# Linear attention and a top-2 expert layer on one Trainium2 core: the last batch and the first expert tiles reordered, output sends put off in the first wave

## The reference

```python
scores = softmax(xn @ gate_w + gate_b)                # per token, 8 experts; the two best are kept
for i in range(n_exp):
    h = relu(xn * w_i @ w1[i] + b1[i])                # 128 -> 512
    y = h @ w2[i] + b2[i]                             # 512 -> 128
    out = where(w_i > 0, y, out)                      # the last chosen expert overwrites
x = x + out
```

## Time and profile before

| | |
|---|---|
| median of three runs | 274.76 us |
| the profiled execution | 274.99 us, of which the span of its instructions is 273.0 us |
| PE busy | 245.6 us (90%), mean granted clock 0.989 |
| DVE, ACT, POOL busy | 195.5, 169.9, 166.0 us |
| DMA queues | 40.57 MB, mean 149 GB/s |

### The profile page before, as it was taken

The page is one execution under the profiler, slowest core; times in us unless marked ns, Lnnn a source line. Parts: engine busy times, 40 slices in busy tenths (PEclk is TensorE's granted clock), DMA queues, the critical chain, the costliest instruction groups (busy, mean ns, idle before and its releaser), DMA issues.

```text
span 273.0 us, 8984 instructions
## 1 busy us (share of the span) xinstructions
PE 245.6 (90%) x3045; PEld 199.5 (73%) x3045; DVE 195.5 (72%) x711; ACT 169.9 (62%) x315; POOL 166.0 (61%) x190
## 2 busy tenths in 40 slices
PE   0989999999999999999999999666998999999993
PEld 0666777777777767767767767435998999999993
DVE  4643466787799899899799798759878655555562
ACT  1386767767767767767777776544456556556550
POOL 6263364564786786786677667850477775455454
PEclk9999999999999999999999999998999999999998
DMA  5799999999600000000000000456666489777500
GB/s 152 227 342 353 352 356 352 352 335 357 196 25 22 2 22 21 2 23 22 2 20 23 2 22 20 116 134 175 185 166 169 119 241 283 180 211 178 150 29 9
DMA packets 31692, 40.57 MB, mean 149 GB/s; under 512 B 3442, under 2 KB 24468, under 8 KB 31648
## 3 DMA queue, kind: packets, MB, share of 16 engines
q1 hardware_dynamic: 29120, 35.69, 43.9%
q0 software_dynamic: 2272, 4.25, 4.5%
q10 hardware_dynamic: 256, 0.07, 0.1%
HBM read 17.98 MB, written 22.48 MB: 148 GB/s over the span
## 4 chain that ended last, share of the span: by engine, by line
PE 69%; ACT 16%; POOL 5%; issue 4%; DVE 3%; DMA 1%; SPq 0%; DVEq 0%; ACTq 0%; POOLq 0%
PE sc L1068 33%; PE p L1068 24%; ACT scores L416 16%; PE av L1068 9%; PE p L1071 3%; POOL expert_rows L594 2%; POOL scores L566 2%; DMA rows<-in_L_attn_hidden_states 1%; POOL out L607 1%; DVE scaled L768 0%; POOL rstd L583 0%; DVE logit L770 0%; DVEq L296 0%; DVE u_sb L718 0%; DVE xn L662 0%
## 5 line engine op out<-in xcount | busy, mean ns | idle before, releaser
L416 ACT ACTIVATE scores<-sc 128x1536 f32<-128x1536 f32 x64 | 92.8, 1451 | 47.0 <-PE sc L1068 47.0
L566 POOL TENSOR_SCALAR_AFFINE_SELECT scores<-scores 128x1024 f32<-128x1024 f32 x64 | 71.3, 1115 | 47.7 <-ACT scores L416 47.1
L1068 PE MATMUL sc<-q_sb,k_sb 32*128 32x256 f32 (+1 forms) x1024 | 60.9, 350 | 10.9 <-ACT scores L416 7.4
L1068 PEld LDWEIGHTS sc<-q_sb,k_sb 32*128 32x128 f32 x1024 | 48.5, 186 | 28.5 <-issue 18.3
L607 POOL DMA_INDIRECT out<-y_sb,xr x39 | 38.4, 983 | 27.6 <-DVE y_sb L1009 22.5
L1068 PE MATMUL av<-scores,v_ext 128*32 128x256 f32 (+1 forms) x1024 | 48.7, 329 | 0.9 <-POOL scores L566 0.9
L516 ACT ACTIVATE hT<-sc,b_sb 128x128 f32<-128x128 f32 x78 | 24.6, 364 | 35.7 <-PE sc L1068 34.9
L1068 PE MATMUL sc<-xwT,w_t 128*128 128x128 f32 x312 | 42.0, 279 | 0.0
L1068 PEld LDWEIGHTS av<-scores,v_ext 128*32 128x32 f32 x1024 | 28.8, 110 | 16.2 <-POOL scores L566 1.4
L997 DVE TENSOR_SCALAR hT<-sc,b_sb 128x128 f32<-128x128 f32 x78 | 23.8, 347 | 21.6 <-PE sc L1068 18.4
L594 POOL DMA_INDIRECT expert_rows<-rows,slot_i x32 | 32.8, 1024 | 10.7 <-issue 7.3
(11 more groups left out here) (136 smaller groups left out, 322.9 us busy)
## 6 DMA issues: line engine op xcount, KB each, us to landing
expert_rows<-pad_rows SPq DMA_DIRECT2D x11, 1572.0 KB, 18.3
w_t<-in_L_ffn_w SPq DMA_DIRECT2D x39, 256.0 KB, 3.5
xr<-expert_rows SPq DMA_DIRECT2D x39, 65.5 KB, 2.7
rows<-in_L_attn_hidden_states SPq DMA_DIRECT2D x16, 128.0 KB, 3.2
out<-y_sb,xr POOLq DMA_INDIRECT x39, 3.0
b_sb<-in_L_ffn_b SPq DMA_DIRECT2D x1, 512.0 KB, 5.8
expert_rows<-rows,slot_i POOLq DMA_INDIRECT x32, 2.4
wo_sb<-in_L_attn_Wo ACTq DMA_DIRECT2D x8, 8.0 KB, 2.4
```

Source lines behind the costliest of these rows:

```text
L416: nc.scalar.activation(scores[g][:, :, :, :].rearrange("p c a t -> p c (a t)"), sc[:, :, 0:SW], ACT.Square, scale=Q_SCALE).then_inc(square ...
L566: nc.gpsimd.affine_select(out=scores[g][:, :, 0:2, :], in_=scores[g][:, :, 0:2, :], compare_op=ALU.is_ge, fill=0.0, base=0, pattern=[[0, G ...
L1068: return nc.tensor.matmul(o, lhsT=l, rhs=r, start=start, stop=stop)
```

## The change

The constants become Y = 20 and DEFER = 12. In the first 12 tiles DVE no longer adds the second bias ahead: `end_y` adds the residual straight from xr, and the bias of tile t - 12 is added (`add_bias`) in the turn of tile t, for t = 12 to 23. POOL sends the results of tiles 0 to 11 only after that, interleaved with those of tiles 12 and up. In the first wave (t < 17) ACT takes three of the four relu chunks and DVE one, and `go_up` writes them to the banks accordingly. In the last period POOL runs the scatters of batches 10 and 11 and `norm2_root(6)` ahead of the four masks of batch 15; DVE and PE load the first table earlier; DVE runs the logits of pair 6 after the loop; PE runs four filler products and puts all four `weigh(15)` behind `project_o(14)`. `project_o(15)` moves from tile 0 to behind the transpose of tile 1, the two last `prefix` from tiles 1 and 6 to 4 and 8, and the late pieces are spread over tiles 0 to 11.

```diff
-    XR, W1, Y, XWT = 20, 6, 10, 4
+    XR, W1, Y, XWT = 20, 6, 20, 4
+    DEFER = 12
+        def low(t):
+            return FC - 1 if t < WAVE else FC // 2
...
 # scalar
-                if p == NB:
-                    exponent(NP - 2)
-                for c in range(FC // 2):
+                for c in range(low(t)):
             normalise(2)
+            exponent(NP - 2)
             act.wait_ge(b1_ready, 1)
-                if t == 3:
+                if t == 4:
                     exponent(NP - 1)
 # gpsimd
             def send_result(t):
-                pool.wait_ge(y_ready, t + 1)
+                if t < DEFER:
+                    pool.wait_ge(y_late, t + 1)
+                else:
+                    pool.wait_ge(y_ready, t + 1)
...
                 if p == NB:
                     scatter(send)
+                    scatter(send + 1)
+                    norm2_root(logits)
                 if core is not None:
                     mask(core, 0)
-                if p == NB:
-                    scatter(send + 1)
...
-            scatter(NB - 4)
-            scatter(NB - 3)
-            for t in range(TILES):
-                if t == 6:
-                    scatter(NB - 2)
-                    scatter(NB - 1)
-                send_result(t)
+            for b in range(NB - 4, NB):
+                scatter(b)
+            for t in range(DEFER, TILES + 1):
+                if t - DEFER < DEFER:
+                    send_result(t - DEFER)
+                if t > DEFER:
+                    send_result(t - 1)
 # vector
                     norm2_stats(tail)
+                if p == NB:
+                    e = experts(dve, 0)
...
-                if logits is not None:
+                if logits is not None and p < NB:
...
             def end_y(t):
                 dve.wait_ge(down_done, t + 1)
-                dve.wait_ge(y_begun, t + 1)
-                nc.vector.tensor_tensor(y_sb[t % Y][:, :], down_bank[t % 2][:, 0:D], y_sb[t % Y][:, :],
+                if t < DEFER:
+                    begun = xr[t % XR][:, 0:D]
+                else:
+                    dve.wait_ge(y_begun, t - DEFER + 1)
+                    begun = y_sb[t % Y][:, :]
+                nc.vector.tensor_tensor(y_sb[t % Y][:, :], down_bank[t % 2][:, 0:D], begun,
                                         ALU.add).then_inc(y_ready, 1)
+            def add_bias(t, e):
+                dve.wait_ge(y_ready, t + 1)
+                nc.vector.tensor_tensor(y_sb[t % Y][:, :], y_sb[t % Y][:, :], b2_sb[:, bass.ds(e * D, D)],
+                                        ALU.add).then_inc(y_late, 1)
...
-            e = experts(dve, 0)
+            route_logits(NP - 2)
             residual(NB - 2)
-            route_sum(NP - 2)
+            norm2_stats(NB - 2)
             spread(NB - 1)
             divide(NB - 1)
-            route_score(NP - 2)
-            route_onehot(NP - 2)
-            norm2_stats(NB - 2)
...
-                begin_y(t, e[t])
+                if t >= DEFER:
+                    begin_y(t, e[t])
+                    if t - DEFER < DEFER:
+                        add_bias(t - DEFER, e[t - DEFER])
                 late_piece(t)
 # tensor
+            def stay_busy(n):
+                for _ in range(n):
+                    mm(p5[:, :], ones[:, :], ones[:, :].unsqueeze(1).broadcast_to([P, 4, P]))
...
+                if p == NB:
+                    stay_busy(4)
+                    e = experts(pe, 0)
                 score_group(core, 3)
-                weigh(core, 0)
-                weigh(core, 1)
+                if p < NB:
+                    weigh(core, 0)
+                    weigh(core, 1)
...
             project_o(NB - 2)
-            weigh(NB - 1, 2)
-            e = experts(pe, 0)
-            weigh(NB - 1, 3)
+            for g in range(GROUPS):
+                weigh(NB - 1, g)
...
                 go_up(t)
-                if t == 0:
-                    project_o(NB - 1)
                 if t + 2 < TILES:
                     transpose_xw(t + 2)
+                if t == 1:
+                    project_o(NB - 1)
                 if t:
                     go_down(t - 1, e[t - 1])
-                if t == 1:
+                if t == 4:
                     prefix(NP - 2)
-                if t == 6:
+                if t == 8:
                     prefix(NP - 1)
```

More of the change, by code:

```diff
@@ L266, in attention_moe_kernel @@
         y_ready = sem("y_ready")
+        y_late = sem("y_late")
         y_out = [sem(f"y_out{i}") for i in range(Y)]
@@ L994, in relu_high @@
                 after(dve, down_done, t - 1)
-                for c in range(FC // 2, FC):
-                    at = (c - FC // 2) * P
+                for c in range(low(t), FC):
+                    at = (c - low(t)) * P
                     ins = nc.vector.tensor_scalar(hT[t % 2][:, c * P:(c + 1) * P], up_bank[t % 2][1][:, at:at + P],
@@ L1015, in late_piece @@
                 if t == 0:
+                    route_ahead(k - 1)
+                    route_sum(k - 1)
+                if t == 1:
                     residual(NB - 1)
                     norm2_stats(NB - 1)
-                if t == 1:
+                if t == 2:
+                    route_best(k - 1)
+                    route_score(k - 1)
+                if t == 3:
+                    route_onehot(k - 1)
+                    route_logits(k)
+                if t == 4:
+                    route_ahead(k)
+                if t == 5:
                     route_place(k - 1)
                     route_taken(k - 1)
-                if t == 2:
+                    route_best(k)
+                if t == 6:
                     route_rows(k - 1)
[L1023 to L1027, removed]
                     route_sum(k)
-                if t == 5:
                     route_score(k)
+                if t == 7:
                     route_onehot(k)
-                if t == 6:
+                if t == 8:
                     route_place(k)
                     route_taken(k)
-                if t == 7:
                     route_rows(k)
+                if t == 9:
                     second_counts(second)
-                if t == 8:
                     dve.wait_ge(left_ready, 1)
                     tiles_before(second)
+                if t == 10:
                     tiles_passed(second)
-                if t == 9:
+                if t == 11:
                     tiles_packed(second)
                     table_done(second, 1, tile_row_b)
-            e = experts(dve, 0)
+            route_logits(NP - 2)
             residual(NB - 2)
-            route_sum(NP - 2)
+            norm2_stats(NB - 2)
             spread(NB - 1)
             divide(NB - 1)
-            route_score(NP - 2)
-            route_onehot(NP - 2)
-            norm2_stats(NB - 2)
             dve.wait_ge(b1_ready, 1)
@@ L1249, in go_up @@
                 for c in range(FC):
-                    at = (c % (FC // 2)) * P
-                    last = mm(up_bank[t % 2][c // (FC // 2)][:, at:at + P], w1_t[t % W1][:, c * P:(c + 1) * P],
+                    high = c >= low(t)
+                    at = (c - high * low(t)) * P
+                    last = mm(up_bank[t % 2][high][:, at:at + P], w1_t[t % W1][:, c * P:(c + 1) * P],
                               xwT[t % XWT][:, :])
```

## The result

The changed kernel took **277.14 us** (median of seven runs, 276.16 to 278.96) against 275.14 for the kernel before in the same runs. The ratio is 1.0099, with a 95% interval from 1.0071 to 1.0126: slower by 1%, some 2.7 us by the ratio and 2.0 by the two medians. The forecast was 276.3, slower by 1.5, from a gain at the front of 5.9 us and a loss behind it of 7.4.

The account below looks back on a forecast made before the run. PE was taken as the limit after a poorly used stretch at 182 to 192 us. A 5.9 us gain and a 7.4 us loss made +1.5, 276.5 on the profiled execution, given as 276.3; range 272.8 to 278.8.

Parts of the forecast that it names:

- a gain at the front: Up to tile 13: the reordered front and the pace behind it bring go_up(13) to 209.9, 5.9 us ahead.
- The sends put off: Tiles 18 to 28: late sends hold back row loads and w1 queued behind them on SP; 7.4 us lost.
- The term from a send to SP's move: From send(11)'s start to SP's row load: taken as 3.7 us, ends 2.1 and 4.3.
- Rival 1: Tiles 18 to 28: the sends do not hold back the loads, the 5.9 us stay, 268.9; chance 0.2.
- The front, up to go_up(2): From batch 15 to tile 2: oT and first rows ready earlier, go_up(2) at 187.7 instead of 192.1, 4.4 us gained.
- The clock: PE in the first tiles: full clock, since PE is never idle longer than about 1 us; about 1.9 us gained.
- Rival 2: First tiles: PE is granted half the clock, +1.9 us, 278.2; chance 0.15.
- Tiles 2 to 13 at 2.0 us: First wave: 11 x 2.0 and two prefixes of 0.2 put go_up(13) at 209.9; three relu chunks on ACT fit.
- DVE beside the masks: Last period: three two-input logits operations cost one mask each, POOL loses nothing, batch 14's statistics end at 181.6.
- The sum: go_up(38) at 209.9 + 37.5 + 19.7 = 267.1 against 265.6: +1.5 us for the whole kernel.

Follow-up runs that it names:

- no_deferral: Changed kernel with DEFER = 0, every send in order, all else of the change kept: 271.59 us, 0.9859 of the kernel before.
- deferral_only: Kernel before with nothing but the deferral of sends and bias (Y = 20, DEFER = 12): 281.29 us, 1.0241 of the kernel before.
- w1_first: Changed kernel with w1 of tile t issued ahead of the row load of tile t + 3 in SP's second wave: 275.82 us, 1.0032 of the kernel before.
- defer_6: Changed kernel with DEFER lowered from 12 to 6: 271.36 us, 0.9878 of the kernel before.
- before_filler: Kernel before with eight filler products between go_up(0) and project_o(15), where PE waits for DVE: 273.53 us, 0.9963 of the kernel before.
- split_some: Changed kernel without deferral, three relu chunks on ACT only in tiles 5 to 8, two elsewhere: 271.82 us, 0.9879 of the kernel before.

## Why the prediction was right, and where its terms were off

- **The sends put off**: right as a mechanism and nearly in size (7.4 forecast, 37.16 - 30.1 = 7.1 in the profile, 5.6 to 6.6 by the times of no_deferral and deferral_only). The term from a send to SP's move is the one that varies: 3.84 here, 2.70 in deferral_only. The gaps are not an even 0.6 either, but eight waits of 0.15 to 1.28. no_deferral, deferral_only and w1_first show it from three sides, defer_6 shows that the count of sends decides. Rival 1 is refuted: w1 was late.
- **The front, up to go_up(2)**: forecast 187.7, profile 188.55. The mechanism is right: the logits run beside the masks, oT is ready at 184.55, PE no longer waits for it. The 0.8 us between are the first rows. The forecast had SP's load of them at 178.7 and 2.3 us to land; here it was issued at 179.23 and ACT waited until 182.42:

```profile
182.42 0.88 ACT L514 ACTIVATE xw<-xr 128x128 f32<-128x128 f32 x2 [3.56 <-DMA xr<-expert_rows]
```

  In eight other traces with this order of scatters ACT began at 180.16 to 181.48, but in split_some's at 183.74. So the forecast's 181 is the usual case, and this execution and split_some's are late ones; no run shows why.
- **The clock**: 1.9 forecast, 1.7 measured by before_filler. Rival 2 did not occur: 1.00 in every stretch from 168 to 192 us, and the filler had no part in that. Why it did not is not shown. The prediction relied on PE being idle for no longer than about 1 us, but in split_some PE stood 1.57 us behind the last group and the clock stayed at 1.00, and in before_filler it stood 1.20 us at that place and the clock was at 0.50 right after. The forecast of a full clock was right, its reason is open.
- **Tiles 2 to 13 at 2.0 us**: this is the step that failed. They took 23.6 us, not 22.2, 2.15 a tile, and 23.3 to 23.5 in the eight other traces with three chunks on ACT in these tiles. "Three relu chunks on ACT make 1.4 us a tile, under 2.0" counts ACT's load, but what matters is when its last piece ends. ACT's timeline at tiles 9 and 10, then PE's at tile 10:

```profile
204.87 0.88 ACT L521 ACTIVATE hT<-sc,b_sb 128x128 f32<-128x128 f32 x3 [0.82 <-PE sc L1095]
205.63 0.27 ACT L509 COPY xwT<-p 128x128 f32<-128x128 f32 x1
205.78 0.52 ACT L514 ACTIVATE xw<-xr 128x128 f32<-128x128 f32 x1
```
```profile
206.35 0.33 PE L1098 MATMUL p<-ident,xw 128*128 128x128 f32 x1
206.90 1.15 PE L1095 MATMUL p<-w_sb,hT 128*128 x8 [0.22 <-issue]
```

  The scaled rows are ready at 206.30, 0.05 before PE's transpose starts, and the next product starts 0.55 us behind that transpose instead of 0.11. In the turns of tiles 3, 10 and 12 the rows were ready 0.05 or 0.06 before the transpose, and the product followed 0.40, 0.55 and 0.48 behind it; in those of 5 and 7 they were ready 0.25 and 0.17 before, and it followed at 0.35 and 0.37; in all others 0.38 or more, and it followed at 0.11 to 0.14. These five tiles take 2.25 to 2.45 us, the other six 1.89 to 2.10. That the late rows are the cause is read from this pattern. In tiles 12 to 17 two runs support it (10.16 and 10.21 us with two chunks, 10.73 with three); in tiles 2 to 12 none isolates it, since with two chunks DVE is late there. So the saved 0.5 us on DVE bought nothing: 23.6 us against 23.75 before.
- **DVE beside the masks**: right. DVE's two sums in the last period and POOL's four masks:

```profile
177.07 1.09 DVE L777 TENSOR_TENSOR scaled<-raw,rstd 128x32 f32<-128x32 f32 x1
178.20 1.03 DVE L779 TENSOR_TENSOR logit<-scaled,gb_sb 128x32 f32<-128x32 f32 x1
```
```profile
177.02 4.28 POOL L572 TENSOR_SCALAR_AFFINE_SELECT scores<-scores 128x1024 f32<-128x1024 f32 x4
```

  Each sum takes as long as a mask, and the four masks 1.07 each, no longer than before. Of the rule of the Trainium skill, "SBUF — State Buffer", section "Who interferes with whom", the half that DVE blocks is seen; the half by which POOL would be held too costs nothing here, and the 0.6 us it would have added is not there. Statistics of batch 14 ended at 181.5, for 181.6.
- **The sum**: gain 3.7 for 5.9, loss 7.1 for 7.4, and 0.4 more behind tile 28 (20.06 us to tile 38; no_deferral's trace has 20.04, so it is not the sends'). That makes +3.8 in this execution against +1.5. Of the pace 1.1 to 1.4 us are in every trace with three chunks. The late rows, and so part of why it is the longest of the seven, are not: the ratio gives +2.7. Of the gain at the front only the whole was measured (3.4 to 3.5 us by the medians of no_deferral) and the fillers, the order of the scatters and the relu split taken singly, which gave nothing clear of the noise; what DVE's and ACT's new orders are worth, each alone, no run shows.

## What to carry to other kernels

When an output transfer is put off, look for what its landing frees: here a buffer whose reload headed an in-order queue, with the weights behind it. Two streams sharing an issuing engine at 1.29 us each lag behind a 2.0 us tile however idle that engine was on average, so count transfers to the last one that something waits for. And when work is shifted to an idle engine, check the end time of what follows it there, not its load.

## What was not expected of the hardware

The clock's fall moved by 4 us between kernels with the same work ahead of it: 0.50 at 189 in the kernel before, 0.50 already from 184 to 186 in before_filler, whose products until 185.5 are the same. The time from SP's issue of the first rows to ACT's start on them varied too, from 1.8 to 3.8 us between the kernels of this front.
